# Layer-0 attention scores in a two-layer model: from six stacked bf16 parts to three float32r products on half the array's rows

## The reference

```
q, k, v = xn @ Wq.T, xn @ Wk.T, xn @ Wv.T           # (4, 512, 256) each
q, k = q * cos + rotate_half(q) * sin, k * cos + rotate_half(k) * sin
scores = einsum('bhqd,bhkd->bhqk', q, k) / sqrt(16)  # per head 512 x 512
attn = einsum('bhqk,bhkd->bhqd', softmax(scores), v)
combined = g * (linear-attention term) + (1 - g) * attn
x + combined @ Wo.T + experts0(xn)
```

## Time and profile before

| | us |
|---|---|
| three runs | 1188.92, 1190.88, 1192.23 (median 1190.88) |
| span of the profiled execution | 1186.0 |
| median less that span | 4.9 |
| busy in the span: PE, PEld | 972.0, 623.9 |
| busy in the span: DVE, ACT, POOL | 584.5, 433.3, 311.8 |

### The profile page before, as it was taken

How to read it: one execution, slowest core, us unless ns; L and a number is a source line. 1 busy time by engine, 2 the same in 40 slices (tenths; PEclk the granted TensorE clock), 3 DMA queues, 4 the chain that set the end, 5 groups by cost and what they waited for, 6 DMA issues and landing times. The chain is left out here.

```text
span 1186.0 us, 16176 instructions
## 1 busy us (share of the span) xinstructions
PE 972.0 (82%) x5323; PEld 623.9 (53%) x5323; DVE 584.5 (49%) x1221; ACT 433.3 (37%) x662; POOL 311.8 (26%) x217
## 2 busy tenths in 40 slices
PE   3699999999589999999998763259999888999871
PEld 2588888888112334444434552235556555665541
DVE  4556566643577785577573322533233333333335
ACT  3435354452245556647646513002222221222210
POOL 3622425153230002012002121033333333333210
PEclk9989999999679998899898877569999999999975
DMA  6713314240523222412321205994322232333352
GB/s 212 224 36 96 110 54 150 54 151 1 145 62 91 66 79 93 145 59 89 133 65 63 98 32 165 274 286 122 109 77 80 80 77 76 85 78 89 81 175 71
DMA packets 150413, 125.47 MB, mean 106 GB/s; under 512 B 63424, under 2 KB 128080, under 8 KB 150352
## 3 DMA queue, kind: packets, MB, share of 16 engines
q1 hardware_dynamic: 146608, 114.45, 32.4%
q0 software_dynamic: 3744, 10.23, 2.9%
HBM read 85.76 MB, written 38.86 MB: 105 GB/s over the span
## 5 line engine op out<-in xcount | busy, mean ns | idle before, releaser
L1075 DVE TENSOR_REDUCE b_negmax<-b_psM 128x1 f32<-128x512 f32 x256 | 163.2, 683 | 75.6 <-PE b_psM L1201 72.6
L1006 ACT ACTIVATE b_probs<-b_psE 128x512 f32<-128x512 f32 x256 | 138.8, 595 | 118.2 <-PE b_psE L1219 117.3
L1201 PE MATMUL b_psM<-b_kst,b_qst 96*128 96x512 bf16 x256 | 98.5, 432 | 27.6 <-DVE b_negmax L1075 13.7
L1219 PE MATMUL b_psE<-b_qst,b_kst 98*128 98x512 bf16 x256 | 89.8, 410 | 15.4 <-ACT b_probs L1006 10.8
L402 POOL TENSOR_TENSOR a_hh<-a_h,a_hh 128x512 fp32r<-128x512 f32 x44 | 57.7, 1312 | 145.5 <-ACT a_hh L455 145.5
L1580 POOL DMA_INDIRECT scratch_ys<-d_y,d_put x39 | 40.2, 1030 | 178.4 <-ACT d_y L1618 176.8
L1847 PE MATMUL d_psG<-d_w,d_xT 128*128 x156 | 80.7, 642 | 4.1 <-issue 3.2
L1855 PE MATMUL d_psU<-d_w,d_xT 128*128 x156 | 79.9, 638 | 0.0
L1219 PEld LDWEIGHTS b_psE<-b_qst,b_kst 98*128 98x128 bf16 x256 | 20.9, 99 | 107.4 <-ACT b_probs L1006 53.8
L1872 PE MATMUL d_psY<-d_w,d_hidden 128*128 x312 | 76.7, 390 | 0.3 <-ACT d_hidden L1612 0.3
L1228 PE MATMUL b_psV<-b_probs,b_vst 128*32 128x512 f32 x512 | 73.6, 648 | 3.2 <-ACT b_probs L1006 3.2
(11 more groups left out here) (310 smaller groups left out, 2174.7 us busy)
## 6 DMA issues: line engine op xcount, KB each, us to landing
scratch_parts<-a_part SPq DMA_DIRECT2D x12, 512.0 KB, 4.0
b_qst<-scratch_parts SPq DMA_DIRECT2D x96, 64.0 KB, 2.3
b_kst<-scratch_parts SPq DMA_DIRECT2D x96, 64.0 KB, 2.3
scratch_parts<-b_part SPq DMA_DIRECT2D x24, 256.0 KB, 3.4
d_qst<-scratch_parts SPq DMA_DIRECT2D x96, 64.0 KB, 2.7
d_kst<-scratch_parts SPq DMA_DIRECT2D x96, 64.0 KB, 2.9
a_cbc<-scratch_cT SPq DMA_DIRECT2D x16, 256.0 KB, 3.9
scratch_v<-a_v SPq DMA_DIRECT2D x4, 1024.0 KB, 4.3
```

The costliest lines, as they stand in the source:

```text
L1006: nc.scalar.activation(probs[k % PSLOTS][:, h, :], psE[h % 2][:, :], ACT.Exp, scale=float(HD) ** -0.5).then_inc(scores_used[h % 2], 1)
L1075: nc.vector.tensor_reduce(negmax[i][:, t, h:h + 1], psM[:, h % 2, :], AX_X, ALU.max, negate=True).then_inc(rows_used[h % 2], 1)
L1201: nc.tensor.matmul(psM[:, h % 2, :], qst[g][0:STACK, h, t * P:(t + 1) * P], kst[g][0:STACK, h, :], start=True, stop=True).then_inc(rows_re ...
L1219: nc.tensor.matmul(psE[h % 2][:, :], kst[g][0:STACKM, h, k * P:(k + 1) * P], qst[g][0:STACKM, h, :], start=True, stop=True).then_inc(score ...
```

## The change

Each rotated value is split in two parts, both float32r (32-bit operands), instead of three bf16 ones. A head's stack is three bands of 16 (`Q_HALF`, `K_HALF`), 48 rows, and 50 with the maximum. Even heads lie from partition 0, odd heads from partition 64, so the two matmuls of a pair stand on the two halves of the array's rows. The order in which PE issues them stays. `second` on ACT and `third` on POOL go, POOL's `rest` writes the second part and no longer waits for `features`; two stores of twice the bytes take the place of three. A group's loads stay 13, with the same bytes in rows twice as long; `send_max` has two loads in place of one. `turn_max` is fp32 through `ident`, its PSUM tile and copy are fp32. The rows of ones in `kst` are set by eight fp32 memsets in place of four bf16 ones, and the last loads of k wait for them in batch 0. `HSLOTS` is 3.

```diff
-HSLOTS = 4
+HSLOTS = 3
+Q_HALF = (0, 0, 1)
+K_HALF = (0, 1, 0)
+ROWS = len(Q_HALF) * HD
+ROWSM = ROWS + 2
+SPLITS = 2
+BAND = 64
@@ layer0_front, POOL: rest, third @@
                     pool.wait_ge(part_done[0], 2 * n + i + 1)
-                    pool.wait_ge(features, 2 * n + i + 1)
-                    nc.gpsimd.tensor_tensor(qk[:, half, :], qk[:, half, :], parts[0][:, half, :],
-                                            ALU.subtract).then_inc(rest_done, 1)
+                    nc.gpsimd.tensor_tensor(parts[1][:, half, :], qk[:, half, :], parts[0][:, half, :].bitcast(F32),
+                                            ALU.subtract).then_inc(part_done[1], 1)
-            steps = {(0, 0): (power,), (8, 0): (rest(0),), (9, 0): (third(0), rest(1)), (10, 0): (third(1),)}
+            steps = {(0, 0): (power,), (8, 0): (rest(0),), (9, 0): (rest(1),)}
@@ layer0_front, ACT @@
-                     (8, 0): (copy_v, copy_xTf), (8, 1): (first(1), second(0)), (9, 0): (copy_kf,), (9, 1): (second(1),)}
+                     (8, 0): (copy_v, copy_xTf), (8, 1): (first(1),), (9, 0): (copy_kf,)}
@@ middle @@
-        qst = [sb(f"qst{g}", [STACKM, HG, SEQ], BF16) for g in range(GROUPS)]
-        kst = [sb(f"kst{g}", [STACKM, HG, SEQ], BF16) for g in range(GROUPS)]
+        qst = [sb(f"qst{g}", [P, HG // 2, SEQ], F32R) for g in range(GROUPS)]
+        kst = [sb(f"kst{g}", [P, HG // 2, SEQ], F32R) for g in range(GROUPS)]
-        psN = ctx.enter_context(nc.psum_tensor("b_psN", [P, SEQ], BF16))
+        psN = ctx.enter_context(nc.psum_tensor("b_psN", [P, SEQ], F32))
@@ middle, SP: load, send_max @@
+                        for c in range(2):
+                            at = BAND * c + i * HD
+                            sp.dma_start(dst[g][at:at + HD, :, :].bitcast(F32), src[c]).then_inc(stack_in[g], 16)
-                sp.dma_start(qst[g][STACK:STACKM, :, :],
-                             scratch["max"].rearrange("(a h) t -> a h t", a=2)).then_inc(max_in[g], 16)
+                for c in range(2):
+                    sp.dma_start(qst[g][BAND * c + ROWS:BAND * c + ROWSM, :, :].bitcast(F32),
+                                 scratch["max"].rearrange("(a j c) t -> c a j t", a=2, c=2)[c]).then_inc(max_in[g], 16)
@@ middle, POOL @@
-                nc.gpsimd.memset(kst[g][STACK:STACKM, :, :], 1.0).then_inc(ones, 1)
+                for c in range(2):
+                    nc.gpsimd.memset(kst[g][BAND * c + 32:BAND * c + ROWSM, :, :].bitcast(F32), 1.0).then_inc(ones, 1)
@@ middle, PE @@
+            def band(h, rows):
+                return slice(BAND * (h % 2), BAND * (h % 2) + rows)
-                    nc.tensor.matmul(psM[:, h % 2, :], qst[g][0:STACK, h, t * P:(t + 1) * P], kst[g][0:STACK, h, :],
-                                     start=True, stop=True).then_inc(rows_ready, 1)
+                    nc.tensor.matmul(psM[:, h % 2, :], qst[g][band(h, ROWS), h // 2, t * P:(t + 1) * P],
+                                     kst[g][band(h, ROWS), h // 2, :], start=True, stop=True,
+                                     tile_position=(BAND * (h % 2), 0)).then_inc(rows_ready, 1)
-                                             nmparts[i][:, t, :, :].rearrange("p a h -> p (a h)"), identb[:, :])
+                                             nmparts[i][:, t, :, :].rearrange("p a h -> p (a h)").bitcast(F32), ident[:, :])
-                        nc.tensor.matmul(psE[h % 2][:, :], kst[g][0:STACKM, h, k * P:(k + 1) * P],
-                                         qst[g][0:STACKM, h, :], start=True, stop=True).then_inc(scores_ready, 1)
+                        nc.tensor.matmul(psE[h % 2][:, :], kst[g][band(h, ROWSM), h // 2, k * P:(k + 1) * P],
+                                         qst[g][band(h, ROWSM), h // 2, :], start=True, stop=True,
+                                         tile_position=(BAND * (h % 2), 0)).then_inc(scores_ready, 1)
```

More of the change, by code:

```diff
@@ L247, in layer0_front @@
         rot = sb("rot", [P, 2 * KT, SEQ])
-        parts = [sb(f"part{i}", [P, 2 * KT, SEQ], BF16) for i in range(3)]
+        parts = [sb(f"part{i}", [P, 2 * KT, SEQ], F32R) for i in range(SPLITS)]
         v32 = sb("v32", [P, TILES, HEADS, VW])
@@ L269, in layer0_front @@
         sined, rotated, min_done, exp_done, features = (sem(n) for n in ("sined", "rotated", "min", "exp", "features"))
-        part_done, rest_done = [sem(f"part{i}") for i in range(3)], sem("rest")
+        part_done = [sem(f"part{i}") for i in range(SPLITS)]
         v_stored, qf_stored, parts_stored, cT_stored = (sem(n) for n in ("v_st", "qf_st", "parts_st", "cT_st"))
@@ L374, in front @@
                 sp.dma_start(scratch["qf"][n].rearrange("k p n -> p k n"), rot[:, 0:KT, :]).then_inc(qf_stored, 16)
-                for i in range(3):
+                for i in range(SPLITS):
                     sp.wait_ge(part_done[i], 2 * n + 2)
-                    sp.dma_start(scratch["parts"][n, i].rearrange("k p n -> p k n"), parts[i][:, :, :]).then_inc(parts_stored, 16)
+                    sp.dma_start(scratch["parts"][n, i].rearrange("k p n -> p k n"), parts[i][:, :, :].bitcast(F32)).then_inc(parts_stored, 16)
             load_x(0, x0_in)
@@ L393, in _ @@
                 front(b + 1)
-            for done, n in ((v_stored, 1), (qf_stored, 1), (parts_stored, 3), (cT_stored, 1)):
+            for done, n in ((v_stored, 1), (qf_stored, 1), (parts_stored, SPLITS), (cT_stored, 1)):
                 sp.wait_ge(done, 16 * n * BATCHES)
@@ L477, in step @@
                     act.wait_ge(rotated, 2 * n + i + 1)
-                    act.wait_ge(parts_stored, 48 * n)
+                    act.wait_ge(parts_stored, 16 * SPLITS * n)
                     nc.scalar.activation(parts[0][:, half, :], qk[:, half, :], ACT.Copy).then_inc(part_done[0], 1)
[L480 to L486, removed]
                 return step
@@ L765, in middle @@
         negmax = [sb(f"negmax{i}", [P, TILES, HG]) for i in range(2)]
-        nmparts = [sb(f"nmparts{i}", [P, TILES, 2, HG], BF16) for i in range(2)]
-        nmT = [sb(f"nmT{i}", [2 * HG, SEQ], BF16) for i in range(2)]
+        nmparts = [sb(f"nmparts{i}", [P, TILES, 2, HG], F32R) for i in range(2)]
+        nmT = [sb(f"nmT{i}", [2 * HG, SEQ], F32R) for i in range(2)]
         outT = sb("outT", [P, GROUPS, SEQ])
@@ L858, in load @@
             def load(b, g):
-                for op, dst, order in ((0, qst, Q_PARTS), (1, kst, K_PARTS)):
+                for op, dst, order in ((0, qst, Q_HALF), (1, kst, K_HALF)):
                     for i, part in enumerate(order):
                         row = (g % 2) * HG * HD
-                        src = scratch["parts"][b, part, KT * op + g // 2, row:row + HG * HD, :]
-                        sp.dma_start(dst[g][i * HD:(i + 1) * HD, :, :],
-                                     src.rearrange("(h d) t -> d h t", d=HD)).then_inc(stack_in[g], 16)
+                        src = scratch["parts"][b, part, KT * op + g // 2, row:row + HG * HD, :].rearrange(
+                            "(j c d) t -> c d j t", c=2, d=HD)
+                        if isinstance(b, int) and b == 0 and op == 1 and i == len(order) - 1:
+                            sp.wait_ge(ones, 2 * g + 2)
+                        for c in range(2):
+                            at = BAND * c + i * HD
+                            sp.dma_start(dst[g][at:at + HD, :, :].bitcast(F32), src[c]).then_inc(stack_in[g], 16)
                 sp.dma_start(vst[g][:, :, :], scratch["v"][b, :, g * HG * VW:(g + 1) * HG * VW]
@@ L1071, in reduce @@
             def reduce(n, i, t):
-                for h in range(HG):
-                    dve.wait_ge(rows_ready, 16 * n + HG * t + h + 1)
+                for at, h in enumerate(range(HG)):
+                    dve.wait_ge(rows_ready, 16 * n + HG * t + at + 1)
                     nc.vector.tensor_reduce(negmax[i][:, t, h:h + 1], psM[:, h % 2, :], AX_X, ALU.max,
@@ L1363, in _ @@
                     turn_max(0, 0)
-            pe.wait_ge(ones, GROUPS)
+            pe.wait_ge(ones, 2 * GROUPS)
             def ready():
```

36 lines of the change are left out of this document (13 added, 23 removed).

## The result

The changed kernel takes 1262.2 us (median of 4 runs, 1260.0 to 1265.6) against 1191.6 of the kernel before on the same chip: a ratio of 1.059, with an interval of 1.056 to 1.062. The forecast was 1208.2, in a range of 1176 to 1230. The sign was right and the size was not: +71 where +17 stood.

The account below looks back on a forecast made before the run. Middle was taken as bound by a loop through engines, each slot closed by PE, DVE, PE in series. Sum: -6.3 - 10.4 + 13.6 + 8.4 + 3 + 9 = +17.3 on 1190.9, 1208.2 us, range 1176 to 1230.

Parts of the forecast that it names:

- the term for the clock: Middle: five more batch 0 slots at 1.2 GHz and two later falls, +9 us; bounds 0 and +27.
- Start of layer0_front: PE's wait near 59 us shrinks, PE starting at about 55.0: -6.3 us, between -2 and -7.
- The 2.2 for a better clock behind the wait: layer0_front: without the idle time, the first products no longer run at the lower clock; 2.2 us of the 6.3 gained.
- The pair: Middle's slots: second scores product of heads 2 and 3 overlaps, about 0.20 a slot, -10.4 us; bounds -12.8 and 0.
- 32-bit loads: Middle: exposed float32r weight loads behind waits, 170 x 0.08 = +13.6 us; bounds 0 and +27.
- maxima: Middle: DVE's copy of the maxima out of PSUM becomes fp32 and longer, +3 us; bounds 0 and +4.
- Shape changes: Middle: array shape changes twice around each of 42 beside steps, 84 x 0.10 = +8.4 us; bounds 0 and +17.
- Slots: Middle at 2.4 GHz: values to values 3.5 or a little more, heads slots 5.0 to 5.3, maxima copy 0.6 to 0.7.
- A held clock: Rival: middle's clock does not fall, the rest as in the sum, 1199.2 us; chance 0.15.
- Faster: Rival: 32-bit loads and shape changes in middle cost nothing, -13.7 to 1177.2 us; chance 0.28.
- No overlap: Rival: paired scores products in middle still run one after the other, 1218.6 us; chance 0.14 shared with the other dearer case.
- Clock down through all of batch 0: Rival: some 14 more batch 0 slots at the lower clock, +18, 1226 us; chance 0.14 shared with the other dearer case.

Follow-up runs that it names:

- the first experiment: Kernel before, bf16 at one position, with row and score products cut from 96 and 98 rows to 48 and 50: 1288.2 us, ratio 1.083.

## Why the prediction was wrong, point by point

**The step that failed is the term for the clock: +9, with a bound of +27; it was about +60.** To part it from the rest I use that the changed kernel and the one with 64 rows a half issue the same instructions at different clocks. In the later batches 332.88 at 0.76 and 304.84 at 0.87 are 2.55 us per hundredth, so about 289.5 at 0.93, 13 over the kernel before; batch 0, 83.86 at 0.58 and 67.39 at 0.88, comes to 65.7 at 0.91, no more than before. These are estimates, take the time as linear in the clock, and rest on clocks of two digits, so they can be off by some 3 us. With the front (-3.8), the prologue (+2.3) and the rest (+1.1), all that isn't the clock is about +13 of the 74.5, where the sum had +8.3. The other 61 or so are the clock.

The mechanism was named in the prediction, with the rows for it. The sizing was wrong in two places. I took five slots of batch 0 and two more falls; in fact batch 0 ran at 0.58, with 13.6 us at 2.4 GHz, and the later batches at 0.76, so that 160 of their 333 us were at 1.2 GHz ((1 - 0.76) / 0.5 of them; 39 us of 276 before). And I priced a slot at the lower level with a quiet one, 1.3; a quiet one of the changed kernel is 1.6 dearer (5.18 against 3.55) and one with `heads` 3.1 (8.39 against 5.29). Most of middle's time has such work beside. The upper bound of 27 was drawn over batch 0 and the first slots behind it, though rows 8 and 9 themselves come from the later batches: nothing in the profile allowed me to stop there.

**Start of layer0_front, -6.3; measured -3.8.** PE goes at 55.60 where I said 55.0, and what is late next is DVE's product, as named. The 2.2 for a better clock behind the wait were there: the first tile's twelve products took 5.10 before, at 0.52, and 2.93 after, at 1.00, so the tile ends 5.7 earlier. Of that 1.4 went again two batches on, where PE has as many products and the clock is 0.97 (175.86 to 240.86 after, 65.00) for 1.00 (181.19 to 244.80 before, 63.61). The sum had the gain right and no term for a fall of the clock further on.

**The pair, -10.4.** Right in its mechanism and its price per quiet slot (0.20 forecast; 0.22 by the slots above, with float32r and with bf16). The Trainium skill, TensorEngine Tiling (Array Packing), Theoretical Speedup, allows 2x for products of so few rows; the two `scores` products within 0.50 agree with that for float32r on two row halves.

**32-bit loads, +13.6, and maxima, +3.** By the same estimate the bf16 pairs (322.40 at 0.74 and 289.25 at 0.88) come to 277.4 at 0.93, against 289.5 for float32r: 12 us in the three later batches, and some 4 in batch 0 (65.7 against 61.2). 16.6 was the sum of both terms. Without pairs the width costs half as much, 6.3.

**Shape changes, +8.4.** Too small. In the bf16 kernel with filled halves `scores` to the `heads` step is 0.32 where `scores` to `rows` is 0.22, and from that step to `rows` it is 1.56 (417.83 to 419.39) for 1.36. That is 0.30 in a slot with `heads`, where I had two changes at 0.10: more than the pair gives there. If the other beside steps cost the same, which is not shown, 42 x 0.30 is 12.6. With 48 pairs at 0.22 the later batches would lose 2.0 by pair and shapes together; the estimate from the bf16 pairs is +1.0 (277.4 against 276.38). Batch 0, which has no step beside, gains 4.2. Together about -3, where the sum had -2.0 for both.

**Slots.** Quiet slots at 3.5 or a little more: 3.55. `heads` slots 5.0 to 5.3: 5.29. Copy of the maxima 0.6 to 0.7: 0.676. Every slot at 2.4 GHz was as forecast. Only how many of them are at 2.4 GHz was not.

**The rivals.** A held clock would have given about 1199 by the prediction, and 1204 by the estimate above (1191 + 13). The kernel with 96 rows, pairs and shape changes taken away, came to 1203. "Faster" needed loads and shapes for nothing; the slots show 0.25 and 0.30 for them. "No overlap" is refuted. "Clock down through all of batch 0" came nearly true, and was the smaller part.

## What to carry to other kernels

Before halving the rows of a product to save PE time, look at what else runs and at the granted clock: a product over fewer rows that takes as long can cost more than it saves, with PE looking busier than before. Price a lower clock by the heaviest slots, not by a quiet one, and carry its bound over every stage in which the changed products run. Rows of zeros made no product longer in these kernels (a bf16 product is 0.39 over 64 rows and over 96), only setting them held middle's start by up to 5 us; padding a stack up to the full height is a cheap try (37 us off the changed kernel, 0.5% off the kernel before).

## What I had not expected of the hardware

PE at 96% busy for 93 us in a row, on 48 rows, stayed at 1.2 GHz all through (batch 0 of the first experiment). Rows of zeros counted as rows: with half of k's 96 rows zero a float32r kernel held 0.92 to 0.93, as the one without zeros. Two float32r products on the two row halves start together and are both done within 0.50 us. A product of zeros in a wait raised the clock where slots are quiet (0.58 to 0.79 and 0.82). Where they are full one a slot did not (0.71 for 0.76 in its one trace) and two did (0.79), and both made the kernel slower; only the first is explained.
